# A two-layer token mixer with experts on one core: the stacked keys come by transfer alone, attention values are divided once per tile, and the set-up and all instruction lists are laid out anew

## The chip, the cores and the metric

The kernel runs on one core of one Trainium2 chip. The metric is the device time of one launch in microseconds (us). A tile is 256 tokens; there are 32 of them.

## The reference, cut to what matters

The input x is 2 sequences of 4096 tokens with 512 channels. All is fp32; E is 8 experts, H 16 heads of 32 channels.

```python
def attn(x, Wk, Wr, Wo, time_decay, time_first):      # RWKV
    k = einsum('btc,hc->bth', x, Wk)
    r = einsum('btc,hc->bth', x, Wr)
    y = wkv_scan(-exp(time_decay), time_first, k, r)  # recurrence over the tokens
    return einsum('bth,ch->btc', sigmoid(r) * y, Wo)

def ffn(x, ...):
    h = rmsnorm(x, gamma1)
    q = (h @ Wq + bq).reshape(b, t, H, HD)
    kv = ((h @ Wdown + bdown) @ Wup + bup).reshape(b, t, H, 2 * HD)
    k, v = split(kv, 2, axis=-1)
    att = softmax(einsum('bthd,btgd->bthg', q, k) / sqrt(HD))   # among the 16 heads of one token
    out = einsum('bthg,btgd->bthd', att, v).reshape(b, t, D)
    x = x + (out @ Wo + bo)
    h2 = rmsnorm(x, gamma2)
    gate = softmax(h2 @ Wg + bg)
    return x + einsum('btd,edf,bte->btf', h2, We, gate)

x = x + attn(layernorm(x), ...)
x = x + ffn(layernorm(x), ...)
```

## The kernel before, in words

**Number format.** Each fp32 operand of a product is split into two fp16 halves, hi (written by ScalarE) and lo (the rest, written by VectorE or GpSimd); a product is three passes on TensorE: hi·hi, lo·hi, hi·lo.

**Steps of a tile.** `mix_*` is the first layer: turn the tokens (`mix_turn`), products K and V (`mix_k`, `mix_v`), the recurrence by scans of VectorE in two halves of the channels (`mix_decay`, `mix_sum`, `mix_value`, `mix_scan`, `mix_rec`, `mix_gate`, `mix_split`, each with h = 0 or 1), and the output product (`mix_project`). `att_*` is the attention: `att_turn`, `att_latent`, `att_q`, `att_up`, then for groups of tokens `att_max` (a first product only to get each row's maximum), `att_m`, eight `att_scores` and eight `att_probs`. `fin_*` is the output product, its norm and the gate. `moe`, 16 pieces of 12 products of 512 columns, is the experts; VectorE adds each piece into `acc` (L1311), and TensorE's piece u waits for VectorE's add of piece u-2, because two PSUM banks take turns.

**Stacks.** For the scores, q and k are copied into the tiles `qs` and `ks` with their halves stacked on the partitions: 32 rows each for `qs` = (hi, hi, lo) and `ks` = (hi, lo, hi). SyncE's queue (SP) issues these as DMAs of 64 KB, each of 64-byte pieces, in `att_up`: eight for the two hi copies of q, four for its lo, four for the lo of k. The two hi copies of k are eight copies on VectorE instead, `att_stack` (L1219).

**Attention values.** Each `att_probs(k)` on VectorE takes the reciprocal of four denominators per partition (L1250), adds the two halves of the values (L1251) and multiplies (L1253). `fin_back` turns the result (L1261).

**Order.** Each engine runs a list written out by hand: HEAD, then ORDER once per tile for i = 4 to 30, then TAIL. An entry is (step, part, lag) and works on tile i - lag; in HEAD the third number is the tile itself. So while tile i is mixed, tile i-1 is in attention and tile i-2 in the experts, all interleaved. Nothing but these lists and the semaphores sets the order.

**Set-up.** The weights are loaded, their maxima give powers of two as scales (three phases: k and r; the other projections; the experts), and they are split to hi and lo. Those of k, r and o1 are first turned on TensorE through PSUM banks (`set_turn`, the bank from `turned(n)`). `set_abs` on ScalarE sums absolute values of the experts' blocks as a bound, `set_times` scales them; GpSimd writes their lo half (L686).

Of the kernel before, what the change touches and what calls it, by code (L numbers as in the profile page):

```python
# [122 lines left out]
def att_before(use):  # L123
# [21 lines left out]
    ("att_scores", 5, 0), ("mix_k", 0, 2), ("att_probs", 4, 0), ("att_scores", 6, 0), ("att_probs", 5, 0),
    ("att_scores", 7, 0), ("mix_v", 0, 2), ("att_probs", 6, 0), ("att_probs", 7, 0), ("att_turn", 0, 1),
    ("fin_project", 0, 0), ("att_latent", 0, 1), ("att_q", 0, 1), ("att_up", 0, 1), ("fin_turn2", 0, 0),
    ("fin_gate", 0, 0), ("att_max", 0, 1), ("att_max", 1, 1), ("att_max", 2, 1), ("att_max", 3, 1), ("moe", 0, 0),
    ("moe", 1, 0), ("att_m", 0, 1), ("moe", 2, 0), ("moe", 3, 0), ("att_scores", 0, 1), ("moe", 4, 0),
# [7 lines left out]
    ("att_scores", 7, 3), ("mix_turn", 0, 1), ("moe", 8, 4), ("att_probs", 6, 3), ("att_probs", 7, 3),  # L157
    ("mix_k", 0, 1), ("mix_v", 0, 1), ("att_turn", 0, 2), ("moe", 9, 4), ("moe", 10, 4), ("att_latent", 0, 2),
    ("att_q", 0, 2), ("moe", 11, 4), ("moe", 12, 4), ("att_up", 0, 2), ("fin_project", 0, 3), ("moe", 13, 4),
    ("moe", 14, 4), ("att_max", 0, 2), ("moe", 15, 4), ("fin_turn2", 0, 3), ("att_max", 1, 2), ("att_max", 2, 2),  # L160
    ("moe", 0, 3), ("att_max", 3, 2), ("fin_gate", 0, 3), ("moe", 1, 3), ("att_m", 0, 2), ("moe", 2, 3),
    ("moe", 3, 3), ("att_scores", 0, 2), ("att_scores", 1, 2), ("moe", 4, 3), ("moe", 5, 3), ("att_probs", 0, 2),
    ("att_scores", 2, 2), ("att_probs", 1, 2), ("att_scores", 3, 2), ("moe", 6, 3), ("att_probs", 2, 2),
    ("att_scores", 4, 2), ("moe", 7, 3), ("att_probs", 3, 2), ("att_scores", 5, 2), ("att_probs", 4, 2),
    ("att_scores", 6, 2), ("mix_project", 0, 1), ("att_probs", 5, 2),
# [1426 lines left out]
```

## Time and profile before

| | |
|---|---|
| median of 3 runs | 2910.02 us (2909.48 to 2913.99) |
| the profiled execution | 2906.95 us |
| its span (first to last instruction) | 2905.1 us |
| TensorE busy | 2618.6 us, 90% |
| VectorE busy | 2453.4 us, 84% |
| ScalarE, GpSimd busy | 1522.6 us, 1006.4 us |

PE is TensorE, DVE VectorE, ACT ScalarE, POOL GpSimd, SP SyncE with its DMA queue. Busy time of PE is the union of its matmuls, with modelled ends.

### The profile page before, as it was taken

What the parts mean: (1) busy time and instruction counts of PE and PEld (TensorE: products, weight loads), DVE (VectorE), ACT (ScalarE), POOL (GpSimd) and SP (SyncE); (2) the same over time, 40 slices, a digit from 0 to 9 for tenths busy, and PEclk for the clock granted to TensorE, in tenths of its full rate; (3) what the DMA queues carried; (4) which work ended last, traced back from release to release, by engine and by line L of the source; (5) the groups of instructions that cost most, each with busy time, mean ns of one, the idle gap of its engine ahead of it and who ended that gap; (6) DMA issues with size and microseconds to landing.
All of it is one profiled execution on the core that took longest, in us unless ns stands there. A gap on an engine that the chain in (4) does not pass through costs nothing.

```text
span 2905.1 us, 49052 instructions
## 1 busy us (share of the span) xinstructions
PE 2618.6 (90%) x18896; PEld 1579.7 (54%) x18896; DVE 2453.4 (84%) x4353; ACT 1522.6 (52%) x2783; POOL 1006.4 (35%) x970
## 2 busy tenths in 40 slices
PE   2447999999999999999999999999999999999899
PEld 2324555555556555555655555555555555565454
DVE  5688888889888888988888898888889888888853
ACT  5664555555555555555555555555555555554531
POOL 0354333334333333433333343333333333333320
PEclk9768999999999999999999999999999999999999
DMA  6011111111111101111110111111011111111110
GB/s 213 15 30 30 38 37 16 29 32 37 38 37 32 21 26 35 37 38 38 23 30 23 38 37 37 37 23 28 26 37 38 38 38 22 26 28 37 30 23 15
DMA packets 579083, 102.51 MB, mean 35 GB/s; under 512 B 547346, under 2 KB 547474, under 8 KB 578834
## 3 DMA queue, kind: packets, MB, share of 16 engines
...
## 4 chain that ended last, share of the span: by engine, by line
PE 54%; DVE 32%; ACT 6%; issue 4%; POOL 2%; SPq 1%; DMA 0%; DVEq 0%; ACTq 0%; POOLq 0%
PE bank L1333 49%; DVE wkv L1134 4%; DVE ks L1219 3%; PE bank L1355 3%; DVE acc L1311 3%; DVE zz L1158 2%; DVE wkv L1123 2%; DVE e L1147 2%; DVE ev L1167 2%; DVE on L1253 2%; DVE zz L1130 2%; DVE mcol L1234 1%; DVE h2t L1096 1%; ACT ot L923 1%; DVE hrow L1225 1%
## 5 line engine op out<-in xcount | busy, mean ns | idle before, releaser
L1333 PE MATMUL bank<-w_e,h2t 128*128 128x512 f16 x6144 | 1392.8, 380 | 72.9 <-DVE acc L1311 52.6
L1333 PEld LDWEIGHTS bank<-w_e,h2t 128*128 128x128 f16 x6144 | 587.3, 98 | 754.6 <-DVE acc L1311 77.1
L1311 DVE SCALAR_TENSOR_TENSOR acc<-bank,gates,acc 128x512 f32<-128x512 f32 x512 | 376.6, 741 | 136.6 <-PE bank L1333 132.3
L727 POOL TENSOR_TENSOR pr<-pr 128x512 f16<-128x512 f32 x256 | 307.1, 1200 | 281.9 <-ACT pr L901 279.2
L899 ACT ACTIVATE pr<-bank,plog,col 128x512 f32<-128x512 f32 x256 | 197.1, 770 | 201.0 <-PE bank L1501 201.0
L1134 DVE TENSOR_TENSOR_SCAN wkv<-e,wkv 128x256 f32<-128x256 f32 x256 | 255.9, 1040 | 22.9 <-ACT e L827 19.6
L696 POOL TENSOR_TENSOR zz<-wkv,zz 128x512 f32<-128x512 f32 x64 | 106.7, 1667 | 432.2 <-DVE ev L1145 432.2
L1333 PE MATMUL bank<-w_o,xo 128*128 128x512 f16 x768 | 176.1, 387 | 49.7 <-DVE xo L1096 49.5
L1158 DVE RECIPROCAL zz<-zz 128x256 f32<-128x256 f32 x128 | 218.5, 1729 | 0.0
L901 ACT ACTIVATE pr<-bank,plog,col 128x512 f16<-128x512 f32 x256 | 197.0, 770 | 0.0
L1333 PE MATMUL bank<-xo,w_k 128*128 128x256 f16 x1536 | 175.6, 275 | 12.0 <-DVE xo L1096 12.0
L1234 DVE TENSOR_REDUCE mcol<-bank 128x4 f32<-128x512 f32 x256 | 160.7, 681 | 19.0 <-PE bank L1488 19.0
L1333 PE MATMUL bank<-w_o,oo 128*128 128x512 f16 x768 | 172.6, 382 | 0.9 <-DVE oo L1096 0.9
L1333 PE MATMUL bank<-xo,w_r 128*128 128x256 f16 x1536 | 172.9, 273 | 0.0
L1333 PE MATMUL bank<-ht,w_q 128*128 128x256 f16 x1536 | 172.9, 273 | 0.0
L1333 PEld LDWEIGHTS bank<-xo,w_k 128*128 128x128 f16 x1536 | 149.2, 99 | 31.6 <-DVE xo L1096 12.9
L1333 PEld LDWEIGHTS bank<-ht,w_q 128*128 128x128 f16 x1536 | 150.3, 98 | 17.4
L1333 PEld LDWEIGHTS bank<-xo,w_r 128*128 128x128 f16 x1536 | 150.2, 98 | 17.4
L1333 PEld LDWEIGHTS bank<-w_o,xo 128*128 128x128 f16 x768 | 73.7, 99 | 141.9 <-DVE xo L1096 55.2
L709 POOL TENSOR_TENSOR x<-x,bo_row 128x512 f32<-128x512 f32 x64 | 92.5, 1466 | 161.8 <-ACT x L854 161.8
L743 POOL TENSOR_TENSOR acc<-x,x 128x512 f32<-128x512 f32 x64 | 80.3, 1276 | 173.1 <-DMA result<-acc 173.1
L714 POOL TENSOR_TENSOR qo<-t,qo 128x256 f16<-128x256 f32 x128 | 109.4, 862 | 84.6 <-ACT qo L884 84.6
...
## 6 DMA issues: line engine op xcount, KB each, us to landing
...
ks<-k SPq DMA_DIRECT2D x128, 64.0 KB, 2.4
...
```

The lines of the kernel that those rows point to most:

```text
L696: nc.gpsimd.tensor_tensor(zz[:, :, :], wkv[:, 2, :, 0:T], zz[:, :, :], ALU.add).then_inc(mix_pool.sem, 1)
L709: nc.gpsimd.tensor_tensor(x2[:, s, :], x2[:, s, :], bo_row[:, :], ALU.add).then_inc(att_pool.sem, 1)
L714: nc.gpsimd.tensor_tensor(grouped(dst, 1)[:, :, b, :], t32[:, b % 2, :].rearrange("p (g j) -> p g j", g=G), grouped(dst, 0)[:, :, b, :], A ...
L727: nc.gpsimd.tensor_tensor(pr16[:, 1, k % 2, :], pr[:, k % 2, :], pr16[:, 0, k % 2, :], ALU.subtract).then_inc(att_pool.sem, 1)
L899: nc.scalar.activation(pr[:, k % 2, :], att_bank[ATT_BANK["S", k]][:, :], ACT.Exp, bias=plog[:, 0:1], scale=colof["soft"])\
L901: nc.scalar.activation(pr16[:, 0, k % 2, :], att_bank[ATT_BANK["S", k]][:, :], ACT.Exp, bias=plog[:, 0:1], scale=colof["soft"])\
L1134: V.tensor_tensor_scan(wkv[:, n, c, 1:T + 1], e1[:, c, :], src[:, c, :], wkv[:, n, c, 0:1], ALU.mult, ALU.add).then_inc(mix_dve.sem, 1)
L1158: V.reciprocal(zz[:, c, :], zz[:, c, :]).then_inc(mix_dve.sem, 1)
L1219: V.tensor_copy(ks[n * HD:(n + 1) * HD, :, f, :], grouped(k16, 0)[f * HD:(f + 1) * HD].rearrange("p g b j -> p g (b j)")).then_inc(att_dve ...
L1234: V.tensor_reduce(mcol[:, 4 * k:4 * k + 4], att_bank[ATT_BANK["M", k]][:, :].rearrange("p (g x) -> p g x", g=4), AX, ALU.max).then_inc(att ...
L1311: V.scalar_tensor_tensor(out=acc[:, s, :], in0=moe_bank[u % 2][:, :], scalar=gates[:, s, e:e + 1], in1=acc[:, s, :], op0=ALU.mult, op1=ALU ...
L1333: ins = nc.tensor.matmul(dst, left(a), right(b), start=(n == 0), stop=(n == last))
```

## The change

1. `att_stack` is gone from VectorE. SP's `att_up` issues eight more DMAs per tile, for rows 0 and 2 of `ks`, between q's lo and k's lo.
2. `att_probs` only adds the two halves, with the denominator as a 33rd column. `fin_back` does one reciprocal of 32 columns and one multiply of 1024 per tile.
3. `set_load` is in five parts, `set_experts` in eight. The turned weights use six PSUM banks in turn in place of two. The bounds of o1 and o2 come from sums of absolute values on ScalarE (four more `set_abs`), no longer from maxima on VectorE.
4. The lists of all five engines have new entries; one line of them is shown.

```diff
-MAXED = ["k", "r", "o1", "q", "o2", "small", "experts"]
+MAXED = ["k", "r", "q", "small", "experts"]
+SUMMED = ["o1", "o2"] + [f"e{e}" for e in range(E)]
+TURN_BANKS = [0, 1, 4, 5, 6, 7]
...
 DVE_HEAD = [
-    ("set_scale", 0, -1), ("set_max", 2, -1), ("set_k", 0, -1), ("set_k", 1, -1), ("set_max", 3, -1),
+    ("set_scale", 0, -1), ("mix_turn", 0, 0), ("set_k", 0, -1), ("set_k", 1, -1), ("set_r", 0, -1), ("set_r", 1, -1),
...
 def turned(n):
-            return bank[n % 2][:, :]
+            return bank[TURN_BANKS[n % len(TURN_BANKS)]][:, :]
...
-        stack_in = Steps(sem("stack_in"), 16, qk=16)
+        stack_in = Steps(sem("stack_in"), 16, qk=24)
...
 def att_up(t, _):                      # SP
-                for src, dst, name, first in ((qo16, qs, "q", (0, 1)), (k16, ks, "k", ())):
-                    rest = 2 if first else 1
+                for src, dst, name, first in ((qo16, qs, "q", (0, 1)), (k16, ks, "k", (0, 2))):
+                    rest = 3 - sum(first)
...
 def set_max(_, n):                     # DVE
                 if name == "small":
+                    dve.wait_ge(summed, 2 * CB)
...
-            def att_stack(t, _):
-                dve.wait_ge(*att_act.done(t, "k"))
-                for f in range(4):
-                    for n in (0, 2):
-                        V.tensor_copy(ks[n * HD:(n + 1) * HD, :, f, :],
-                                      grouped(k16, 0)[f * HD:(f + 1) * HD].rearrange("p g b j -> p g (b j)")).then_inc(att_dve.sem, 1)
...
 def att_probs(t, k):                   # DVE
-                V.reciprocal(rden[:, 4 * k:4 * k + 4], pv[:, :, HD]).then_inc(att_dve.sem, 1)
-                V.tensor_reduce(og, pv.rearrange("p g (l d) -> p g d l", l=2)[:, :, 0:HD, :], AX, ALU.add).then_inc(att_dve.sem, 1)
-                dve.wait_ge(*att_dve.done(t, "norm", 3 * k + 1))
-                V.tensor_tensor(og, og, rden[:, 4 * k:4 * k + 4].unsqueeze(2).to_broadcast([P, 4, HD]), ALU.mult).then_inc(att_dve.sem, 1)
+                V.tensor_reduce(on[:, 4 * k:4 * k + 4, :], pv.rearrange("p g (l d) -> p g d l", l=2), AX, ALU.add).then_inc(att_dve.sem, 1)
...
 def fin_back(t, _):                    # DVE
+                V.reciprocal(rden[:, :], on[:, :, HD]).then_inc(fin_dve.sem, 1)
+                dve.wait_ge(*fin_dve.done(t, "den"))
+                V.tensor_tensor(on[:, :, 0:HD], on[:, :, 0:HD], rden[:, :].unsqueeze(2).to_broadcast([P, G, HD]), ALU.mult).then_inc(fin_dve.sem, 1)
+                dve.wait_ge(*fin_dve.done(t, "quot"))
```

What the lists do to the order, at three places. First TensorE, within one tile of the steady part, from the query product (w_q) to the gate product (w_g): `w_e` are experts' pieces of 12, `w_u` is `att_up`, `w_o<-oo` is `fin_project`, `ident,ot` is `fin_turn2`, `ks,qs` of 8 is one `att_max`. Before:

```order
L1333 MATMUL bank<-ht,w_q 128x256 x48
L1333 MATMUL bank<-w_e,h2t 128x512 x24
L1471 MATMUL bank<-c,w_u 128x256 x16
L1333 MATMUL bank<-w_o,oo 128x512 x24
L1333 MATMUL bank<-w_e,h2t 128x512 x24
L1488 MATMUL bank<-ks,qs 128x128 x8
L1333 MATMUL bank<-w_e,h2t 128x512 x12
L1355 MATMUL bank<-ident,ot 128x128 x8
L1488 MATMUL bank<-ks,qs 128x128 x16
L1333 MATMUL bank<-w_e,h2t 128x512 x12
L1488 MATMUL bank<-ks,qs 128x128 x8
L1333 MATMUL bank<-w_g,h2t 128x8 x24
```

And of the change:

```order
L1333 MATMUL bank<-ht,w_q 128x256 x48
L1333 MATMUL bank<-w_e,h2t 128x512 x12
L1471 MATMUL bank<-c,w_u 128x256 x16
L1333 MATMUL bank<-w_e,h2t 128x512 x24
L1333 MATMUL bank<-w_o,oo 128x512 x24
L1333 MATMUL bank<-w_e,h2t 128x512 x36
L1355 MATMUL bank<-ident,ot 128x128 x8
L1487 MATMUL bank<-ks,qs 128x128 x16
L1333 MATMUL bank<-w_g,h2t 128x8 x24
L1333 MATMUL bank<-w_e,h2t 128x512 x12
L1487 MATMUL bank<-ks,qs 128x128 x16
```

The first use of the stacks (`ks,qs`) moved behind all experts' pieces of the older tile and behind the turn, and only half of it stands ahead of the gate.

Second VectorE, in the same stretch: from the gated output's second operand to the add of pieces 14 and 15. `ks<-k` is `att_stack`, `wkv<-wcol` to `zz<-e` is `mix_decay`, `mcol` is `att_max`. Before:

```order
L1118 COPY wkv<-carry 128x6
L1123 SCALAR_TENSOR_TENSOR wkv<-wcol,wkv,xk 128x256 x2
L1126 TENSOR_TENSOR e<-xk,wkv 128x512
L1130 TENSOR_SCALAR zz<-e,ucol 128x256 x2
L1219 COPY ks<-k 32x32x32 x8
L1225 STREAM_TRANSPOSE hrow<-ht 128x1024
L1271 SCALAR_TENSOR_TENSOR x<-bank,col,x 128x512 x2
L1311 SCALAR_TENSOR_TENSOR acc<-bank,gates,acc 128x512
L1229 TENSOR_TENSOR vp<-hrow,vp 128x32x32
L1234 TENSOR_REDUCE mcol<-bank 128x4 x2
L1311 SCALAR_TENSOR_TENSOR acc<-bank,gates,acc 128x512 x2
L1096 SCALAR_TENSOR_TENSOR h2t<-bank,h2t 128x512 x2
```

And of the change:

```order
L1225 STREAM_TRANSPOSE hrow<-ht 128x1024
L1311 SCALAR_TENSOR_TENSOR acc<-bank,gates,acc 128x512 x2
L1104 SCALAR_TENSOR_TENSOR xo<-ev,col,xo 128x512
L1229 TENSOR_TENSOR vp<-hrow,vp 128x32x32
L1271 SCALAR_TENSOR_TENSOR x<-bank,col,x 128x512 x2
L1311 SCALAR_TENSOR_TENSOR acc<-bank,gates,acc 128x512
L1126 COPY wkv<-carry 128x6
L1131 SCALAR_TENSOR_TENSOR wkv<-wcol,wkv,xk 128x256 x2
L1134 TENSOR_TENSOR e<-xk,wkv 128x512
L1138 TENSOR_SCALAR zz<-e,ucol 128x256 x2
L1311 SCALAR_TENSOR_TENSOR acc<-bank,gates,acc 128x512 x2
L1104 SCALAR_TENSOR_TENSOR h2t<-bank,h2t 128x512 x2
```

The copies are gone, and the transpose of the values and the output's add (L1271) now stand ahead of the second half's `mix_decay`.

Third VectorE at the start of the program: the first tile's lo half (`xo<-bank`). Before, it stands behind the experts' scales (`ee`):

```order
L1090 SCALAR_TENSOR_TENSOR w_o<-bank,scl,w_o 128x512 x4
L1004 TENSOR_TENSOR mx<-mx,gam 128x4 x8
L977 TENSOR_REDUCE bound<-mx 128x8
L1079 TENSOR_SCALAR pw<-bound 128x8
...
L1038 TENSOR_SCALAR ee<-pw 128x8 x2
L1096 SCALAR_TENSOR_TENSOR xo<-bank,xo 128x512 x2
```

And of the change:

```order
L1060 TENSOR_SCALAR wcol<-ecol 128x4
L1104 SCALAR_TENSOR_TENSOR xo<-bank,xo 128x512 x2
L1098 SCALAR_TENSOR_TENSOR w_k<-bank,scl,w_k 128x512 x4
L1098 SCALAR_TENSOR_TENSOR w_r<-bank,scl,w_r 128x512 x4
...
L984 TENSOR_REDUCE mx<-bvcol 128x1
L1012 TENSOR_TENSOR mx<-mx,gam 128x4 x3
L984 TENSOR_REDUCE bound<-mx 128x9
L1126 COPY wkv<-carry 128x6
```

It moved to right behind the first scales, and the first tile's recurrence begins behind the second phase's bounds instead of behind the experts'. The loads keep their order on SP up to the constants; then come the first two experts, the first residual, four experts, the second tile's x (which waits for the first tile's second `mix_decay`), and only then the last two experts.

## Rows read from the trace of the kernel before

**Rows 1.** The chain that ended last, by line, over the whole run.

```profile
PE bank L1333 49%; DVE wkv L1134 4%; DVE ks L1219 3%; PE bank L1355 3%; DVE acc L1311 3%; DVE zz L1158 2%; DVE wkv L1123 2%; DVE e L1147 2%; DVE ev L1167 2%; DVE on L1253 2%; DVE zz L1130 2%; DVE mcol L1234 1%; DVE h2t L1096 1%; ACT ot L923 1%; DVE hrow L1225 1%
```

**Rows 2.** Stretches: length, busy of PE, PEld, DVE, ACT, POOL, clock, DMA share, GB/s.

```profile
0.00:258.19 258.19, 109.14 (x794) 80.91 (x795) 182.86 (x343) 155.46 (x310) 86.61 (x90) 0.79 0.28 77
258.19:2696.00 2437.81, 2319.34 (x16887) 1398.29 (x16886) 2146.30 (x3789) 1297.00 (x2346) 867.37 (x827) 1.00 0.16 32
2696.00:2858.86 162.86, 147.93 (x1004) 81.21 (x1003) 109.58 (x200) 69.92 (x127) 49.97 (x51) 0.97 0.15 25
```

**Rows 3.** Timeline of PE: start, length; a turn, an expert piece, a query product.

```profile
1019.49 1.09 PE L1355 MATMUL bank<-ident,ot 128*128 128x128 f32 x8 [0.21 <-ACT ot L923]
...
1022.21 2.77 PE L1333 MATMUL bank<-w_e,h2t 128*128 128x512 f16 x12 [0.74 <-DVE h2t L1096]
...
1078.52 5.40 PE L1333 MATMUL bank<-ht,w_q 128*128 128x256 f16 x48
```

**Rows 4.** What PE waited for, 258.19 to 2696: us in total, times, longest.

```profile
PE bank L1333 <- DVE acc L1311: 52.6, 55, 2.0
PE bank L1512 <- DVE on L1251: 22.2, 28, 0.8
PE bank L1333 <- DVE h2t L1096: 21.8, 28, 1.5
PE bank L1333 <- DVE xo L1096: 13.9, 27, 0.5
```

**Rows 5.** Groups, 300 to 2700: busy us, mean ns, then idle before them.

```profile
L1311 DVE SCALAR_TENSOR_TENSOR acc<-bank,gates,acc 128x512 f32<-128x512 f32 x450 | 330.6, 740 | 77.2 <-PE bank L1333 73.3 <-issue 0.7
L1134 DVE TENSOR_TENSOR_SCAN wkv<-e,wkv 128x256 f32<-128x256 f32 x228 | 228.6, 1043 | 12.2 <-ACT e L827 9.1
L1158 DVE RECIPROCAL zz<-zz 128x256 f32<-128x256 f32 x113 | 193.2, 1730 | 0.0
L1234 DVE TENSOR_REDUCE mcol<-bank 128x4 f32<-128x512 f32 x224 | 141.0, 681 | 18.8 <-PE bank L1488 18.8
L1253 DVE TENSOR_TENSOR on<-on,rden 128x128 f32<-128x128 f32 x224 | 115.3, 515 | 7.7
L1219 DVE COPY ks<-k 32x1024 f16<-32x1024 f16 x224 | 94.3, 421 | 6.1
L1147 DVE TENSOR_TENSOR e<-e,v 128x512 f32<-128x512 f32 x57 | 65.6, 1152 | 0.0
L1250 DVE RECIPROCAL rden<-bank 128x4 f32<-128x4 f32 x224 | 37.8, 169 | 0.4 <-PE bank L1513 0.4
L1229 DVE TENSOR_TENSOR vp<-hrow,vp 128x1024 f16<-128x1024 f32 x28 | 34.1, 1218 | 0.0
```

**Rows 6.** Timeline of SP's queue in one tile: start, length of the issuing.

```profile
1085.90 5.65 SPq L648 DMA_DIRECT2D qs<-qo  x8
...
1094.46 2.82 SPq L652 DMA_DIRECT2D ks<-k  x4
```

**Rows 7.** The stretch of that burst, columns as in rows 2.

```profile
1087.00:1098.00 11.00, 11.00 (x60) 5.76 (x59) 9.99 (x19) 6.12 (x13) 3.36 (x5) 1.00 0.75 90
```

**Rows 8.** Start of the program on DVE and POOL: timeline, idle before.

```profile
34.70 0.16 DVE L977 TENSOR_REDUCE mx<-bqcol 128x1 f32<-128x4 f32 x1 [3.78 <-DMA bg_row<-in_ffn_bg]
65.33 1.29 DVE L1096 SCALAR_TENSOR_TENSOR xo<-bank,xo 128x512 f16<-128x512 f32 x2
71.86 1.40 DVE L1123 TENSOR_TENSOR_SCAN wkv<-wcol,wkv,xk 128x256 f32<-128x256 f32 x2 [0.27 <-ACT xk L807]
...
189.40 4.50 POOL L686 TENSOR_TENSOR w_e<-w_e 128x512 f16<-128x512 f32 x4
```

**Rows 9.** Start of the program on PE: timeline.

```profile
112.50 7.98 PE L1333 MATMUL bank<-w_o,xo 128*128 128x512 f16 x24 [33.53 <-DVE xo L1096]
177.14 1.03 PE L1501 MATMUL bank<-qs,ks 106*128 106x128 f16 x8 [3.57 <-DMA qs<-m]
258.19 6.84 PE L1333 MATMUL bank<-w_e,h2t 128*128 128x512 f16 x24
```

More of the change, by code:

```diff
@@ L145 @@
[L145 to L149, printed above, removed]
@@ new lines @@
+    ("att_probs", 6, 0), ("att_probs", 7, 0), ("mix_k", 0, 2), ("att_turn", 0, 1), ("mix_v", 0, 2),
+    ("att_latent", 0, 1), ("att_q", 0, 1), ("fin_project", 0, 0), ("att_up", 0, 1), ("fin_turn2", 0, 0),
+    ("fin_gate", 0, 0), ("att_max", 0, 1), ("att_max", 1, 1), ("att_max", 2, 1), ("moe", 0, 0), ("att_max", 3, 1),
+    ("moe", 1, 0), ("moe", 2, 0), ("att_m", 0, 1), ("moe", 3, 0), ("moe", 4, 0), ("att_scores", 0, 1),
+    ("att_scores", 1, 1), ("moe", 5, 0), ("att_probs", 0, 1), ("att_scores", 2, 1), ("moe", 6, 0),
@@ L154 @@
+    ("att_probs", 1, 1), ("att_scores", 3, 1), ("att_probs", 2, 1),
 ]
 PE_ORDER = [
[L157 to L165, printed above, removed]
+    ("att_scores", 4, 3), ("moe", 7, 4), ("att_probs", 3, 3), ("att_scores", 5, 3), ("moe", 8, 4),
@@ new lines @@
+    ("moe", 9, 5), ("mix_turn", 0, 2), ("att_probs", 6, 4), ("att_probs", 7, 4), ("moe", 10, 5), ("mix_k", 0, 2),
+    ("mix_v", 0, 2), ("att_turn", 0, 3), ("fin_project", 0, 4), ("att_latent", 0, 3), ("att_q", 0, 3),
+    ("att_up", 0, 3), ("moe", 11, 5), ("moe", 12, 5), ("moe", 13, 5), ("fin_turn2", 0, 4), ("moe", 14, 5),
+    ("moe", 15, 5), ("fin_gate", 0, 4), ("att_max", 0, 3), ("att_max", 1, 3), ("att_max", 2, 3), ("att_max", 3, 3),
+    ("moe", 0, 4), ("att_m", 0, 3), ("moe", 1, 4), ("moe", 2, 4), ("moe", 3, 4), ("att_scores", 0, 3),
@@ new lines @@
+    ("att_latent", 0, 2), ("att_q", 0, 2), ("att_up", 0, 2), ("fin_project", 0, 3), ("moe", 12, 4), ("moe", 13, 4),
+    ("moe", 14, 4), ("moe", 15, 4), ("fin_turn2", 0, 3), ("fin_gate", 0, 3), ("att_max", 0, 2), ("att_max", 1, 2),
+    ("att_max", 2, 2), ("att_max", 3, 2), ("moe", 0, 3), ("att_m", 0, 2), ("moe", 1, 3), ("moe", 2, 3),
+    ("att_scores", 0, 2), ("att_scores", 1, 2), ("moe", 3, 3), ("att_probs", 0, 2), ("att_scores", 2, 2),
+    ("att_probs", 1, 2), ("att_scores", 3, 2), ("moe", 4, 3), ("att_probs", 2, 2), ("att_scores", 4, 2),
@@ L225 @@
+    ("att_vlo", 0, 1), ("mix_split", 0, 2), ("mix_decay", 1, 2), ("fin_turn2", 0, 0), ("att_max", 0, 1),
 ]
 DVE_ORDER = [
[L228 to L231 removed]
@@ new lines @@
+    ("att_stats", 0, 3), ("att_norm", 0, 3), ("moe", 10, 5), ("fin_back", 0, 4), ("mix_decay", 0, 2),
+    ("att_turn", 0, 3), ("mix_sum", 0, 2), ("mix_value", 0, 2), ("att_latent", 0, 3), ("fin_project", 0, 4),
+    ("mix_scan", 0, 2), ("mix_rec", 0, 2), ("mix_rec", 1, 2), ("moe", 11, 5), ("mix_gate", 0, 2), ("moe", 12, 5),
+    ("moe", 13, 5), ("mix_split", 0, 2), ("mix_decay", 1, 2), ("att_vt", 0, 3), ("moe", 14, 5), ("moe", 15, 5),
+    ("mix_sum", 1, 2), ("fin_turn2", 0, 4), ("att_vlo", 0, 3), ("att_max", 0, 3), ("att_max", 1, 3),
```

435 lines of the change are left out of this document (213 added, 222 removed), and 3 rows, old and new, of the table POOL_HEAD.

## The prediction

> **What bounds the kernel now.** First the chain that ended last [rows 1]: half of it is the experts' products on PE, but the rest is a string of VectorE lines, each 1 to 4%, among them the key copies `ks` with 3% and the divided values `on` with 2%. So neither engine bounds alone; they take turns. Next the busy time by stretch [rows 2]. Up to 258.19 us, where the first expert piece of tile 0 starts [rows 9], PE works 109 of 258 us: that is the filling. From there to 2696 PE is busy 2319.3 of 2437.8 us, so 118.5 are idle. Tile 9's first piece starts at 1022.21 [rows 3], so a tile takes (1022.21 - 258.19) / 9 = 84.9 us, the stretch holds 28.7 tiles, and a tile is 80.8 us of work and 4.1 of idle. That 4.1 is all that a better order can win per tile. Who ends the idle [rows 4], over 28: the adds into `acc` 1.9, `on` 0.8, `h2t` 0.8, `xo` 0.5 us, and 0.1 to 0.2 of small ones. Every large one is VectorE being late. Its busy time in the same stretch is 2146 us, 74.8 a tile [rows 2].
>
> **VectorE's work.** Per tile the change removes the eight copies, 94.3 / 28 = 3.4 us, the reciprocals, 37.8 / 28 = 1.35, and the multiplies, 115.3 / 28 = 4.1 [rows 5]. It adds one reciprocal of 32 columns: between the 128x4 (0.17) and the 128x256 one (1.73) the slope is 6.2 ns a column, so 0.34 us; one multiply of 1024 columns, nearest row the 128x1024 subtraction with 1.22 us; the eight adds have 33 values for 32, 0.1 together. Net -7.2 us. This is no gain by itself: it counts only where PE waits for VectorE, at most the 4.1.
>
> **Where the multiply goes.** The old 128x128 multiply averages 515 ns, more than a twelfth of the 1218 ns row per column, eight times within the scores' phase, in which GpSimd writes the lo halves. The Trainium skill, "SBUF — State Buffer", section on the two separate sides, says that a VectorE operation with two SBUF inputs and a GpSimd one exclude each other for the whole instruction; the excess fits it. By that rule the new multiply, which stands where GpSimd is mostly idle, costs 1.2 and not 8 x 0.5; the sum has 1.2 either way, from its row.
>
> **The stacks.** SP issues 24 transfers in place of 16. Eight took 5.65 us and the last four 2.82, so one is 0.70 us [rows 6], and eight more are 5.65. The query product ended at 1078.52 + 5.40 = 1083.9 [rows 3], SP began 2.0 later. The new list has `mix_exp` and `att_latent` of ScalarE ahead of q after a later V product, which I put at 0.7 more. Landing is then 2.7 + 24 x 0.70 + 1.5 = 21.0 us after the query product; the 1.5 is from the last issue (1097.3) to the end of that burst's traffic, with DMA at 0.75 to 1098 [rows 7]. PE has before its first use of the stacks: six expert pieces of 2.6 (2.77 less the overlap with the next), `att_up` 1.8 (16 products where q's 5.40 has 48), `fin_project` 5.2 (24 of a piece's products), the turn 1.0 [rows 3], together 23.6. The slack is 2.6 us: hidden, but it is the thinnest cover of the change. Nothing else in SP's queue is hurt: the x load and the store come after.
> A page speaks against these transfers: the Trainium skill, "DMA: Bandwidth & Descriptors", Specifications, wants 512 bytes or more for line rate, and these are 64-byte pieces. The trace agrees on the rate, 90 GB/s in the burst; by the rate alone 24 x 64 KB would take 17.5 us, about what issuing takes, so the sum stays.
>
> **The decisive stretch.** It runs from the end of `h2t`'s lo half, T. PE before: gate, moe 0, then on. PE after, from T to the start of piece 5: gate 0.6, five pieces 13.0, four `att_max` halves 0.9, `att_m` and two scores 0.7 = 15.2. VectorE after, to the add of piece 3, which piece 5 needs: two maxima 1.4 twice and once more twice (8 x 0.68 less overlap = 5.1), gate 1.7 (eight small operations, the smallest row being 0.17), four adds 3.0, first scans 1.4 to 2.1, `att_m` 0.6, value products 1.3 to 1.8 = 13.1 to 14.3. In time. Then scans 2.1 to 3.1, reciprocal 1.73, add 0.74 [rows 5]: 17.7 to 19.9 (21 with GpSimd in the way as in the 1152 ns row), against PE's start of piece 6 at 15.2 + 2.6 + 0.45 = 18.25. Wait 0 to 2.5, I take 1.0 where before it was 1.9. After that each step has a slack of 0.3 to 2 us. `h2t` keeps its 0.8: turn, ScalarE, VectorE in a row with the same 0.9 of maxima as cover. For `on`, `xo`, the start of the next tile and the store (now behind an x load, which leaves it a slack of about 0.3 before `acc` is needed) I put 0.7 together, bounds 0.2 to 1.5. Sum 2.5 us of idle a tile, bounds 1.1 to 4.1. Gain 1.6 x 28.7 = 46 us, bounds 0 to 86.
>
> **The filling.** Tile 0's lo half waits at 65.33 behind all expert loads, and its scans start at 71.86 [rows 8]. In the new list what holds them is the last constant, at 34.70 [rows 8], so about 35.5: 36 earlier. From there on ScalarE has seven pairs of expert sums ahead of tile 0's tanh (+3), and its sums of the last two experts, loaded only after tile 0's second `mix_decay`, come ahead of the second tanh: tile 0's output product starts near 80 instead of 112.50 [rows 9], 32 earlier. Three weight splits moved behind it cost 5.1, the longer stack 5.7. GpSimd then has five experts in a row (4.50 each [rows 8] and 0.6 for ScalarE's hi before it, 26 us) ahead of tile 1's denominators; with these the first scores start near 151 instead of 177.14: 26 earlier. From the first scores to the first expert piece were 81.1 us [rows 9]; the new order needs about 66 plus some waits, I take 71. So the first piece is 36 us earlier, near 222. Bounds: 18 (the expert chain of ScalarE and GpSimd runs on into the scores) and 48 (66 us, no waits).
>
> **The end.** 2696 to 2858.86 has 14.9 us of PE idle [rows 2]. Less VectorE work gives 3 back; but in the tail list tile 29 has only four pieces, the turn and the gate between its query product and its stacks (about 16 us against 21) and tile 30 has 19: +4. Net +1, bounds -5 to +8.
>
> **Sum.** 46 + 36 - 1 = 81 us off 2906.95, 2826 for such an execution; the runs' median stands 3.1 above it, so 2829.
>
> **Rivals.**
> (a) VectorE's stretch stays as late as before, as the new POOL list puts `mix_num` before the first scores' lo: idle stays 4.1, 2875. For it: the acc waits moved, not removed, have only 0.3 to 1.5 us of slack. Against: 3.4 us of copies are gone from right before the stretch.
> (b) The order comes out as planned, idle falls to 1.1, and the filling gives 42: 2910 - 86 - 42 + 1 = 2783.
> (c) The stacks land 2 us beyond the slack each tile, because ScalarE ends q late: +57, 2886. It decides from 2.6 us.
> (d) Slower: 24 transfers in one queue do not keep 0.70 us but take 0.95 each, landing 6.0 later, 3.4 beyond the slack and 97 us in sum, and the filling gives only its 18: 2910 - 46 - 18 + 97 + 1 = 2944. It needs over 0.90 us each to eat the gain. Against: no growth from the first eight to the last four [rows 6], and the DMA share of 0.75 leaves room [rows 7].
> (e) The filling gives nothing since the expert chain ends when it did: 2865.
>
> **Numbers.** Likeliest 0.50, own range 2795 to 2860; (a) 0.13; (b) 0.15; (c) 0.11; (d) 0.05; (e) 0.06. The range 2780 to 2884 takes in (b), (a), (e) and the likeliest, and leaves out most of (c) and (d). A measurement of this kernel tells about 0.2% from no change, 5.8 us: faster 0.93, same 0.02, slower 0.05.
>
> **What would show it.** Right: per tile near 83.3 us; L1219 gone, no wait of PE for `ks` in the steady stretch; acc waits near 1 us a tile, at piece 6; VectorE busy near 68 a tile; first expert piece near 222. Wrong: PE waiting for DMA `ks`; a tile over 84; the first piece after 240; SP rows of k's hi above 6 us for eight.

## The result, and the profile after

| | before | after |
|---|---|---|
| time, median of 4 runs, us | 2910.86 (2909.48 to 2913.99) | 2759.11 (2758.60 to 2760.13) |
| profiled execution: span, us | 2905.1 | 2756.5 |
| first expert piece of tile 0, us | 258.19 [rows 9] | 229.15 |
| a tile in the steady stretch, us | 85.05 | 80.58 |

The changed kernel takes 0.9478 of the time before, 95% interval 0.9461 to 0.9494: 151.8 us less, where 81 were forecast and 2780 was the range's lower end. Direction right, size wrong by 70 us. A tile is the mean of 22, between the 7th and the 29th start of the first layer's output product. Times here and below are medians of undisturbed executions; the profile of `maxima_first` alone is of a disturbed one, and none of its rows is read.

The page of the changed kernel, busy time and then the chain that ended last, by engine:

```profile
PE 2586.4 (94%) x18896; PEld 1580.4 (57%) x18896; DVE 2133.6 (77%) x3647; ACT 1531.3 (56%) x2799; POOL 948.9 (34%) x970
...
PE 88%; DVE 4%; ACT 4%; POOL 2%; SPq 1%; issue 1%; DMA 0%; ACTq 0%; DVEq 0%; POOLq 0%
```

VectorE is nearly out of the chain: what was a string of its lines [rows 1] is 4% now, and PE bounds. The stretches, columns as in [rows 2]:

```profile
0.00:229.15 229.15, 101.09 (x785) 76.80 (x786) 157.04 (x310) 163.07 (x333) 87.88 (x90) 0.74 0.38 95
229.15:2578.57 2349.42, 2317.23 (x17046) 1417.20 (x17045) 1885.78 (x3186) 1315.35 (x2374) 818.74 (x839) 1.00 0.23 40
```

This stretch has 32 us of idle, but its first and last tiles are longer than the others. The split per tile is read from the 22 even tiles, before and then after, both with the same number of matmuls (589 a tile):

```profile
625.71:2496.85 1871.14, 1777.28 (x12958) 1072.31 (x12959) 1655.53 (x2905) 996.10 (x1805) 669.47 (x638) 1.00 0.16 32
580.22:2353.09 1772.87, 1755.48 (x12962) 1075.37 (x12960) 1437.21 (x2421) 1000.19 (x1805) 622.41 (x638) 1.00 0.23 40
```

Divided by 22, PE's busy time was 80.8 us a tile and is 79.8, its idle was 4.3 and is 0.8. So 3.5 came from idle and 1.0 from time that the trace counts as busy. Who ends the idle in the longer stretch, as in [rows 4]:

```profile
PE bank L1333 <- DVE h2t L1104: 25.0, 29, 3.4
PE bank L1333 <- DVE acc L1311: 1.8, 2, 1.2
```

`on` and `xo` are gone, the `acc` waits (52.6) nearly, and only `h2t` is as it was: 0.74 us a tile. One tile on PE: two starts of the output product, one period apart; between them the query product, the first use of the stacks, the gate, piece 0 and what follows it, and pieces 5 and 6:

```profile
902.56 5.34 PE L1333 MATMUL bank<-w_o,xo 128*128 128x512 f16 x24
...
924.49 5.40 PE L1333 MATMUL bank<-ht,w_q 128*128 128x256 f16 x48
...
953.07 1.06 PE L1487 MATMUL bank<-ks,qs 104*128 104x128 f16 x16
954.87 0.76 PE L1333 MATMUL bank<-w_g,h2t 128*128 128x8 f16 x24 [0.74 <-DVE h2t L1104]
955.49 2.75 PE L1333 MATMUL bank<-w_e,h2t 128*128 128x512 f16 x12
958.08 1.06 PE L1487 MATMUL bank<-ks,qs 104*128 104x128 f16 x16
...
969.89 2.75 PE L1333 MATMUL bank<-w_e,h2t 128*128 128x512 f16 x12
...
973.13 2.75 PE L1333 MATMUL bank<-w_e,h2t 128*128 128x512 f16 x12
...
983.14 5.34 PE L1333 MATMUL bank<-w_o,xo 128*128 128x512 f16 x24
```

Piece 0 ends at 958.24, and the product behind it starts 0.16 us before that. By these modelled ends work that follows without a wait overlaps with what is ahead of it; work that follows a wait does not.

The decisive stretch in that tile, on VectorE and on GpSimd beside it:

```profile
966.24 0.67 DVE L1155 TENSOR_TENSOR e<-e,v 128x512 f32<-128x512 f32 x1
...
967.79 1.44 DVE L1142 TENSOR_TENSOR_SCAN wkv<-e,wkv 128x256 f32<-128x256 f32 x2
...
969.35 1.74 DVE L1166 RECIPROCAL zz<-zz 128x256 f32<-128x256 f32 x1
971.01 0.65 DVE L1311 SCALAR_TENSOR_TENSOR acc<-bank,gates,acc 128x512 f32<-128x512 f32 x1
```

```profile
966.39 1.65 POOL L703 TENSOR_TENSOR zz<-wkv,zz 128x512 f32<-128x512 f32 x1 [3.94 <-DVE ev L1153]
969.31 1.09 POOL L707 TENSOR_TENSOR ev<-wkv,ev 128x512 f32<-128x512 f32 x1 [1.27 <-DVE wkv L1142]
```

The add that piece 6 needs is done at 971.66, and PE comes for it at 973.13: VectorE is 1.5 us early, and this is its slack there. Groups of the steady stretch, where [rows 5] had 1043, 1152 and 8 x 515 ns:

```profile
L1142 DVE TENSOR_TENSOR_SCAN wkv<-e,wkv 128x256 f32<-128x256 f32 x228 | 185.6, 855 | 66.3 <-ACT e L834 65.4
L1155 DVE TENSOR_TENSOR e<-e,v 128x512 f32<-128x512 f32 x57 | 52.1, 915 | 0.0
L1259 DVE TENSOR_TENSOR on<-on,rden 128x1024 f32<-128x1024 f32 x30 | 36.8, 1225 | 1.0
L1257 DVE RECIPROCAL rden<-on 128x32 f32<-128x32 f32 x30 | 10.4, 347 | 0.0
```

SP's queue in that tile, as in [rows 6], and the start on PE, as in [rows 9]:

```profile
932.24 5.65 SPq L655 DMA_DIRECT2D qs<-qo  x8
...
940.79 6.73 SPq L655 DMA_DIRECT2D ks<-k  x8
947.56 2.81 SPq L659 DMA_DIRECT2D ks<-k  x4
```

```profile
81.79 8.30 PE L1333 MATMUL bank<-w_o,xo 128*128 128x512 f16 x24 [46.88 <-DVE xo L1104]
...
140.63 3.79 PE L1487 MATMUL bank<-ks,qs 104*128 104x128 f16 x32 [18.71 <-DMA ks<-k]
...
158.86 1.04 PE L1500 MATMUL bank<-qs,ks 106*128 106x128 f16 x8 [2.83 <-DMA qs<-m]
...
222.60 1.97 PE L1355 MATMUL bank<-ident,ot 128*128 128x128 f32 x8 [11.45 <-ACT ot L930]
```

The issuing ends 20.5 us after the query product (929.89), PE's first use is 23.2 after it, without a wait. This tile is one of 6 in 32 in which the keys' first eight took over 6 us; in the others they took 5.6 to 5.9.

### The profile page after: what moved, and what is told of

It reads as the page before. It is cut to its first block, busy times and chain, and to the rows that moved or that the text cites. A ratio compares the mean times of both kernels' runs of the same rounds, so it can differ in the third digit from the quotient of the medians.

```text
span 2756.5 us, 48625 instructions
## 1 busy us (share of the span) xinstructions
PE 2586.4 (94%) x18896; PEld 1580.4 (57%) x18896; DVE 2133.6 (77%) x3647; ACT 1531.3 (56%) x2799; POOL 948.9 (34%) x970
## 4 chain that ended last, share of the span: by engine, by line
PE 88%; DVE 4%; ACT 4%; POOL 2%; SPq 1%; issue 1%; DMA 0%; ACTq 0%; DVEq 0%; POOLq 0%
PE bank L1333 78%; PE bank L1355 3%; PE bank L1500 2%; PE bank L1471 2%; PE bank L1511 2%; DVE h2t L1104 1%; PE bank L1487 1%; POOL w_e L693 1%; ACT h2t L939 1%; PE bank L1512 1%; ACT ot L789 1%; DVE mcol L1234 0%; ACT t L888 0%; POOL pr L734 0%; DVE acc L1311 0%
## 5 line engine op out<-in xcount | busy, mean ns | idle before, releaser
L734 POOL TENSOR_TENSOR pr<-pr 128x512 f16<-128x512 f32 x256 | 295.7, 1160 | 182.3 <-ACT pr L908 180.9
L1142 DVE TENSOR_TENSOR_SCAN wkv<-e,wkv 128x256 f32<-128x256 f32 x256 | 210.8, 864 | 74.6 <-ACT e L834 73.4
L750 POOL TENSOR_TENSOR acc<-x,x 128x512 f32<-128x512 f32 x64 | 80.3, 1276 | 261.5 <-DMA result<-acc 261.5
L1249 DVE TENSOR_REDUCE on<-bank 128x132 f32<-128x264 f32 x256 | 103.3, 424 | 74.3 <-PE bank L1512 74.3
L703 POOL TENSOR_TENSOR zz<-wkv,zz 128x512 f32<-128x512 f32 x64 | 94.1, 1470 | 158.4 <-DVE ev L1153 158.3
```

What stands on the lines that cost most here:

```text
L703: nc.gpsimd.tensor_tensor(zz[:, :, :], wkv[:, 2, :, 0:T], zz[:, :, :], ALU.add).then_inc(mix_pool.sem, 1)
L734: nc.gpsimd.tensor_tensor(pr16[:, 1, k % 2, :], pr[:, k % 2, :], pr16[:, 0, k % 2, :], ALU.subtract).then_inc(att_pool.sem, 1)
L1142: V.tensor_tensor_scan(wkv[:, n, c, 1:T + 1], e1[:, c, :], src[:, c, :], wkv[:, n, c, 0:1], ALU.mult, ALU.add).then_inc(mix_dve.sem, 1)
L1249: V.tensor_reduce(on[:, 4 * k:4 * k + 4, :], pv.rearrange("p g (l d) -> p g d l", l=2), AX, ALU.add).then_inc(att_dve.sem, 1)
```

## The experiments

Theory at this point: the operations unload VectorE, the lists turn that into time and cover the longer transfers; idle of PE costs more than the trace shows as idle. Rivals: the operations alone carry it; or the lists alone. The period is the mean of the same 22 tiles in every kernel, with PE's busy and idle time in it; a wait is idle of over 0.15 us ahead of an instruction of PE.

**Operations and lists apart.** `ops_only` is the kernel before with both operations and its own lists; `division_only_old_lists` has the division alone; the others start from the changed kernel and put one or both old operations back. One line of each is shown; with the copies go 16 transfers again:

```
 DVE lists:    ("att_vt", ..)  ->  ("att_stack", ..), ("att_vt", ..)             copies_back
-(k16, ks, "k", (0, 2))                     +(k16, ks, "k", ())
-V.tensor_reduce(on[..], pv.., AX, ALU.add)                                    # division_back
+V.reciprocal(rden[..], pv[:, :, HD]); V.tensor_reduce(og, ..); V.tensor_tensor(og, og, rden.., ALU.mult)
```

> The kernel before with the two changed operations alone (both key copies by transfer, one division a tile); its own lists, two turning banks and set-up, the copies' entries dropped from the lists. Theory 1, the operations carry the steady gain: VectorE's 7.2 us a tile are what PE waited for, idle falls from 4.1 to near 1 and the tile to 80.6 to 81.5, with nothing from the filling: 2785 to 2815. Theory 2, the lists carry it: h2t's, xo's and most acc waits stay where the old order puts them, the tile stays near 83 to 83.5: 2850 to 2875. A first expert piece near 258 either way.

> The kernel before with one division a tile and nothing else: copies on VectorE, 16 transfers, old lists. With both operations it was 3018, with PE waiting 4.1 us a tile for the transferred keys. Theory 1, that loss was the longer transfer queue alone, and VectorE's relief is worth something by itself: the `on` waits of 0.8 a tile go and the acc waits shrink, tile 83.5 to 84.3, 2865 to 2890. Theory 2, the relief is worth nothing without a new order: 2905 to 2913.

> The changed kernel with the eight key copies back on VectorE (3.4 us a tile, ahead of the V transpose) and 16 stack transfers. Theory A, VectorE has slack under the new lists (it idles 16 of 80.6 us a tile): under 0.5 us a tile, 2755 to 2775. Theory B, each us taken off VectorE came back as time: 3.4 x 28 = 95 us, near 2850. In between, if the stretch behind the copies (value products, fin's x2, decay, the turn) has under 3.4 us of slack: 1 to 2 us a tile, 2790 to 2815.

> The changed kernel with reciprocal and multiply per four heads again, in the scores' phase. It adds 3.8 us of VectorE a tile there at the old durations, where VectorE waits 2.2 us a tile for the PV products. Theory A, slack: under 1 us a tile, 2760 to 2785. Theory B, one for one: 2860. If the small multiplies take 0.5 us because GpSimd writes the probabilities' lo halves in the same phase, their row reads 450 ns or more again under these lists; if it was the old order's doing, under 300.

> The changed kernel with both old operations back, so set-up, banks and lists alone. Theory 2, the lists carry the gain: 2780 to 2810. Theory 1, the operations carry it: 2860 or more, the filling's 29 us being all that stays. If both are needed, that is if the lists only pay when VectorE is 7 us shorter, this one and the one with operations alone each lose more than half of the gain of 151: both above 2835.

| kernel | lists | division | keys | us | period | busy | idle | waits a tile |
|---|---|---|---|---|---|---|---|---|
| before | old | old | copied | 2910.86 | 85.05 | 80.8 | 4.3 | 6 |
| `division_only_old_lists` | old | new | copied | 2861.04 | 83.17 | 80.2 | 2.9 | 4 |
| `ops_only` | old | new | transferred | 3018.15 | 88.75 | 81.9 | 6.9 | 4 |
| `lists_only` | new | old | copied | 2830.23 | 82.46 | 80.5 | 2.0 | 4 |
| `copies_back` | new | new | copied | 2796.63 | 81.33 | 80.0 | 1.3 | 2 |
| `division_back` | new | old | transferred | 2793.94 | 81.68 | 80.3 | 1.4 | 3 |
| after | new | new | transferred | 2759.11 | 80.58 | 79.8 | 0.8 | 1 |

Most of these missed their theories. `division_only_old_lists` came 4 us under theory 1, `lists_only` between its two, `division_back` 9 above theory A and far from B; `copies_back` is in the range of its middle case, though its tile is 0.74 longer and not 1 to 2. Both theories for `ops_only` missed: it is 107 us slower than before. First PE's waits in its stretch 258 to 2696, then one tile's first use of the keys:

```profile
PE bank L1477 <- DMA ks<-k: 111.9, 27, 4.7
```

```profile
1046.10 0.62 PE L1477 MATMUL bank<-ks,qs 104*128 104x128 f16 x8 [4.68 <-DMA ks<-k]
```

The query product ended there at 1024.14, so the keys land 22.0 after it, while the old list brings PE to them after 17.3. The transfers that cost 157 us under the old lists (3018 against 2861) win 36 and 37.5 under the new ones (2830 to 2794, 2797 to 2759). That is rival (c) and (d)'s place, with another cause: no slower transfers, but a list that reaches for them too early. PE waits 4.2 us a tile for them, and the period is 5.6 longer than without the transfers; the granted clock, at 0.98 in these tiles, has a part in the rest. The division, in contrast, pays under either: 50 us under the old (its `on` and `xo` waits are gone, its `acc` waits still 53.1), 34 and 35 under the new. Set-up, banks and lists with the old operations are worth 81, with the first expert piece at 236.8 where it was 258.2. No run takes these three apart. So neither rival holds: the lists alone give 81 of the 152, the two operations behind them 71, and the two operations without them lose 107.

So theory A, slack, fell for both operations under the new lists as well, and so did B: 3.4 us of copies a tile cost 0.74, 3.8 us of division 1.09. The busy time goes with the waits: 79.8 with one a tile, 80.0 with two, 80.2 to 80.5 with three or four, 80.8 with six. The multiply is 535 ns a piece in `division_back`. Which of them are long is seen with GpSimd's queue beside them:

```profile
908.64 0.72 DVE L1253 TENSOR_TENSOR on<-on,rden 128x128 f32<-128x128 f32 x1
...
911.37 0.29 DVE L1253 TENSOR_TENSOR on<-on,rden 128x128 f32<-128x128 f32 x1
```

```profile
907.71 2.67 POOL L734 TENSOR_TENSOR pr<-pr 128x512 f16<-128x512 f32 x2 [1.88 <-ACT pr L908]
911.53 1.16 POOL L734 TENSOR_TENSOR pr<-pr 128x512 f16<-128x512 f32 x1 [1.15 <-ACT pr L908]
```

0.29 alone, 0.72 while GpSimd works. Copies are hit too: tile 0's eight take 9.03 us in `copies_back` for 3.4, GpSimd being at the experts, and its first piece comes at 236.1 in place of 229.2.

**The slack of the stacks.**

```
-for f, n: sp.dma_start(ks[n.., :, f, :], k16 block f)
+for f, n: two transfers, groups 0 to 15 and 16 to 31          # 32 in place of 24, the same bytes
```

> The changed kernel with each of the eight transfers of the key's hi half issued as two of half the size, so 32 stack transfers in place of 24 with the same bytes. It measures the slack of the stacks under the new lists: the query product's end to PE's first use is 23.2 us, and with the old lists 24 transfers land 22.0 after it. Theory 1, the slack is 1.2 us and an issue costs what it did whatever its size (0.70): landing 5.6 later, PE waits for the keys 4.4 us a tile, 2760 + 125 = 2885. Theory 2, an issue costs by its pieces (0.35 for half the size): nothing changes, 2760. By the forecast's slack of 2.6 and a full 0.70 each: 3.0 a tile, 2845.

Measured: 2908.34, 23 us above theory 1. Sixteen half transfers take as long each as whole ones, and PE waits 99.1 us in 27 tiles, 3.7 each. Issuing ends 25.2 after the query product where it was 20.1 (means of 21 tiles), so the slack was 5.1 - 3.7 = 1.4 us, not 2.6; the 1.2 ahead of this run was close. First SP's row and PE's wait in one tile, then PE's clock in two stretches of 4 us behind it, the last column but two:

```profile
1493.42 10.76 SPq L656 DMA_DIRECT2D ks<-k  x16
```

```profile
1508.77 1.65 PE L1488 MATMUL bank<-ks,qs 104*128 104x128 f16 x16 [3.42 <-DMA ks<-k]
```

```profile
1508.00:1512.00 4.00, 3.23 (x43) 2.54 (x44) 2.76 (x6) 1.44 (x3) 0.00 (x0) 0.63 0.86 205
1512.00:1516.00 4.00, 4.00 (x30) 2.22 (x29) 0.90 (x6) 0.22 (x1) 2.42 (x2) 0.94 0.19 70
```

After 3.4 us of idle the granted clock falls to the lower of its two levels (1.2 of 2.4 GHz) for about 3 us, by the two means. The period is 85.1 us, 4.5 more for 3.7 of wait.

**The slack of VectorE, and what a wait costs.** Unused reciprocals (1.73 each) behind the second scans, ahead of the add that piece 6 needs, two and then one:

```
 mix_scan, h == 1:   +for c in range(2): V.reciprocal(e2[:, c, :], v32[:, HF + c, :])
```

> The changed kernel with two more 128x256 reciprocals on VectorE (3.47 us a tile, results not used) behind the second scans, in the decisive stretch, ahead of the add that piece 6 waits for. The profile gives that add a slack of 1.5 us there. Theory 1, slack as read: PE waits about 2.0 us a tile at piece 6 and the tile is 82.7, 2760 + 60 = 2820. Theory 2, lateness feeds itself because a late VectorE meets GpSimd's probabilities' lo halves again (scans above 950 ns on average): 3.5 or more a tile, above 2860. Theory 3, the slack behind takes it all up: under 2775.

> The changed kernel with one more 128x256 reciprocal (1.73 us a tile, result not used) where vector_delay had two. With two the wait at piece 6 was 1.99, so the slack is 3.47 - 1.99 = 1.48. Theory 1, one leaves a wait of 0.25 plus about 0.15 of drain a tile and the granted clock stays at its full value: tile 80.9 to 81.1, 2768 to 2776. Theory 2, any wait there is amplified as with two (2.8 us for 2.0): 0.35 to 0.4 and no more, the same numbers, but with the clock under 1.00 in the steady stretch. Theory 3, lateness of VectorE as such costs what it costs with two, half of 85: 2800.

Measured 2844.31 and 2777.55. PE's rows at piece 6: two tiles with two reciprocals, the clock behind the second of them, and a tile with one:

```profile
1419.80 2.76 PE L1336 MATMUL bank<-w_e,h2t 128*128 128x512 f16 x12 [1.94 <-DVE acc L1314]
...
1502.46 4.36 PE L1336 MATMUL bank<-w_e,h2t 128*128 128x512 f16 x12 [1.92 <-DVE acc L1314]
```

```profile
1504.00:1508.00 4.00, 4.00 (x33) 2.10 (x32) 3.31 (x5) 0.63 (x1) 0.00 (x0) 0.64 0.00 0
```

```profile
1544.59 2.76 PE L1335 MATMUL bank<-w_e,h2t 128*128 128x512 f16 x12 [0.30 <-DVE acc L1313]
```

One leaves a wait of 0.30, so the slack was 1.43, as read. A typical tile takes 81.06, 0.48 more: the wait costs 0.18 beyond itself, near the 0.16 of overlap that it takes away. With two the wait is 1.9 on average and the period 83.4, 2.8 more, between theories 1 and 2. The two rows tell why: behind 1.94 us of idle the clock stays and the tile takes 82.7, 2.1 more for 1.9 of wait, as a short wait would; behind 1.92 it falls, piece 6 takes 4.36 us in place of 2.75 and the tile 84.4. It fell in 11 of 25 tiles, and nothing in the rows tells which. The scans stay at 858 ns, so theory 2 with its GpSimd is out.

**GpSimd beside the scans.**

```
 mix_sum (GpSimd), h == 1, behind the denominators (not shown: waits for pr16 to be free, and for the two to be done):
+for c in range(2): nc.gpsimd.tensor_tensor(pr16[:, 1, c, :], wkv[:, 2, :, 0:T], wkv[:, 2, :, 0:T], ALU.subtract)
```

> The changed kernel with two more 128x512 subtractions on GpSimd (2.3 us a tile, results not used) behind the second denominators, where the second scans of VectorE run (two in 1.44 us; before, 3.13 with GpSimd at work beside them). Theory 1, the two engines keep each other out: the second scans' mean rises from 855 to about 1100 ns (the pair by 1.0 to 1.7 us), piece 6 loses most of its 1.5 us slack, 2760 to 2790. Theory 2, the old length came from something else in the old order: the mean stays within 20 ns, 2760.

Measured 2786.97, in the range of theory 1, but by another wait than the one it names. VectorE's second scans, GpSimd beside them, and what PE then waits for:

```profile
1548.58 2.47 DVE L1149 TENSOR_TENSOR_SCAN wkv<-e,wkv 128x256 f32<-128x256 f32 x2
```

```profile
1549.08 2.80 POOL L709 TENSOR_TENSOR pr<-wkv 128x512 f16<-128x512 f32 x2
```

```profile
1554.31 0.19 PE L1518 MATMUL bank<-vp,pr 128*128 128x66 f16 x1 [0.95 <-POOL pr L741]
```

The pair takes 2.47 for 1.44, as theory 1 has it; the mean over both halves rises only to 942, since the first pair is untouched. Piece 6 has the slack for it; of the 28 us, 24 are the wait for the first probabilities' lo half (28 times in the steady stretch), which stands behind the two subtractions. So this run shows that GpSimd lengthens the scans, and not what longer scans cost. PE's busy time stays at 79.8 here with two waits a tile: at that place no product overlapped before either (piece 5 ends at 972.64 in the changed kernel, the next product starts at 972.69). The page of the Trainium skill "SBUF — State Buffer", section on the two separate sides, says that of a VectorE operation with two SBUF inputs and a GpSimd one that reads SBUF, the one that starts first holds the shared port for its whole instruction. The scans agree: they take 1.09 and 1.46 us one by one, the second ending 0.55 behind the subtraction that had started before it.

**The one wait left.** Piece 0 ahead of the gate in the steady list, its blocks 0 and 1 waiting for the first half of `h2t` only:

```
-("att_max", 1, 2), ("fin_gate", 0, 3), ("moe", 0, 3),
+("att_max", 1, 2), ("moe", 0, 3), ("fin_gate", 0, 3),
+ahead = {2 * b: fin_dve.done(t, "h2_lo", b) for b in range(2)}       # waited for ahead of blocks 0 and 2
```

> The changed kernel with expert piece 0 ahead of the gate's product in the steady list, its first half waiting only for the first lo half of h2t and its second half for the second. PE's one wait left, 0.74 us for h2t, and the 0.15 of drain behind it go; the gate comes 2.4 us later on PE, but VectorE was at the maxima until 0.4 us before. Theory 1, the wait is what is left to win: the tile falls by 0.8, 2735 to 2742. Theory 2, VectorE's adds are then late by the gate's shift and piece 2 waits for add 0: the same within 3 us, 2757 to 2763.

Measured 2748.29 (2742.94 to 2748.93), ratio to before 0.9437 (0.9423 to 0.9451): the fastest of the kernels run (two below are within 0.5 us of it), 11 us below the changed one, half of what theory 1 gave. PE's row:

```profile
1513.01 2.75 PE L1335 MATMUL bank<-w_e,h2t 128*128 128x512 f16 x12 [0.23 <-DVE h2t L1104]
```

The wait is 0.23 and not zero, because the first lo half itself ends there, and the period is 80.15, 0.43 less and not 0.8.

**The filling.** Four turning banks in place of six; then, step by step, what is ahead of tile 0's first scores: expert splits 5 to 7 behind them on GpSimd, with ScalarE's hi halves of 6 and 7 later too (`late_experts`), the maxima ahead of tile 1's sums on VectorE (`maxima_first`, alone), both and ScalarE's normalised rows earlier (`filling_reordered`), ScalarE's last scalings behind the scores too (`scalings_late`). Three of these also with piece 0 first.

```
-TURN_BANKS = [0, 1, 4, 5, 6, 7]            +TURN_BANKS = [0, 1, 4, 5]
 POOL_HEAD: -.. ("set_e5", ..), ("set_e6", ..), ("mix_sum", 1, 1), ..    # late_experts
            +.. ("att_scores", 7, 0), .. ("set_e5", ..), ("att_stats", 0, 1), ("set_e6", ..), ("set_e7", ..)
 DVE_HEAD:  -("mix_sum", 1, 1), ("att_max", 3, 0), ("att_m", 0, 0)       # maxima_first
            +("att_max", 3, 0), ("att_m", 0, 0), ("mix_sum", 1, 1)
```

> The changed kernel with four turning banks in place of six. With six, PE turns the first weights without a wait by 23.8 us, but tile 0's output product starts at 81.79 and waits for VectorE all the time since. Theory 1, VectorE's and ScalarE's own work up to there sets that start and the banks only let PE be early: within 2 us, 2757 to 2761. Theory 2, earlier turning starts the splits earlier: the output product 4 to 10 us later, 2763 to 2769.

> The changed kernel with the splits of experts 5, 6 and 7 behind the first scores on GpSimd (and the hi halves of 6 and 7 on ScalarE later too), and ScalarE's exponentials of tile 1's second half ahead of expert 5's. Theory 1, the expert chain on GpSimd, which runs without a pause from 128.3 to 159.1 us, is what holds the first scores' lo halves and so the filling's missing 7 us: the first scores' product at 150 to 153 in place of 158.9, the first expert piece at 219 to 224 in place of 229.2, 2748 to 2754. Theory 2, the stacks' landing at 140.6 and what follows it set the filling: within 2 us of 2759.

> The changed kernel with VectorE's second half sums of tile 1 behind tile 0's last maxima and `att_m` in the filling, instead of ahead of them, where they wait 3.05 us for ScalarE. Theory 1, this order holds tile 0's scores: their product starts at 151 to 153 in place of 158.86. Theory 2, GpSimd's expert chain to 159.1 holds the lo halves anyway: the first probabilities' product stays at 165, and the time within 2 us of 2759.

> late_experts plus the maxima first on VectorE and tile 0's normalised rows ahead of the last expert scalings on ScalarE. All three holds of the first scores that the profile shows are gone: the stacks at 141 are then the first limit, the scores' product at 150 to 152, the first probabilities' product near 156 in place of 165.3. If that passes through to the end, 8 us: near 2751. If experts 6 and 7, now split while tile 1's latents are made, take it back (in late_experts the turn of tile 0's output waited 3.4 us longer and came 2.3 later), 2756 to 2761.

> filling_reordered with ScalarE's scalings of experts 6 and 7 and the hi halves of expert 5 moved behind the first scores as well (7 us of ScalarE). Theory 1, they were the last hold of the probabilities: the first probabilities' product at 157 to 159 in place of 164.1 and the first expert piece 5 to 6 us earlier than 231.5: 2752 to 2756. Theory 2, from the scores on the filling is set by other work (ScalarE between tile 1's keys and tile 0's norms, and the 24 transfers of tile 1, which end at 224.5 in the changed kernel): the probabilities come earlier, the first piece does not, 2758 to 2762.

> Both: expert splits late and piece 0 ahead of the gate. If the filling and the steady stretch add up, 2748 less what the late experts gave: 2737 to 2744 by theory 1, 2746 to 2750 by theory 2.

> The same with piece 0 ahead of the gate in the steady list: 10 to 11 us below filling_reordered, so 2740 if the filling gives its 8 us, 2746 to 2750 if it doesn't.

> The same with piece 0 ahead of the gate in the steady list: 10 to 11 us below scalings_late by either theory, 2742 to 2746 by theory 1, 2747 to 2751 by theory 2.

| | us | scores' product | first probabilities | turn of tile 0's output |
|---|---|---|---|---|
| after | 2759.11 | 158.86 | 165.27 | 222.60 |
| `four_turn_banks` | 2759.17 | 158.14 | 164.53 | 220.92 |
| `late_experts` | 2760.58 | 158.19 | 164.32 | 224.93 |
| `maxima_first` | 2760.56 | not read | | |
| `filling_reordered` | 2760.33 | 154.64 | 164.10 | 224.86 |
| `scalings_late` | 2759.21 | 154.42 | 160.47 | 222.72 |

With piece 0 first: 2748.67, 2750.18 and 2748.72. Kernels with one and the same filling place the first expert piece between 227.5 and 230.1, so less than some 2 us in this table says nothing. Not one of these steps moves the time, though the last brings the probabilities 4.8 us forward. PE in `scalings_late`:

```profile
160.47 0.21 PE L1520 MATMUL bank<-vp,pr 128*128 128x66 f16 x1 [5.01 <-POOL pr L732]
...
222.72 1.97 PE L1364 MATMUL bank<-ident,ot 128*128 128x128 f32 x8 [12.93 <-ACT ot L928]
...
229.34 4.01 PE L1342 MATMUL bank<-w_e,h2t 128*128 128x512 f16 x12
```

Tile 1's output product starts at 170.69, 4.8 us earlier than in the changed kernel, and the turn of tile 0's output waits for ScalarE until 222.7 all the same. What is won ahead of the scores is taken back behind them.

## Why the prediction was right or wrong

The measured 2759 lies below the range and below every rival. Counted from expert piece to expert piece, tile 27's was at 2553.28 and is at

```profile
2406.02 2.75 PE L1333 MATMUL bank<-w_e,h2t 128*128 128x512 f16 x12
```

So the 27 tiles from tile 0's took 2295.1 us and take 2176.9: 118 won where 1.6 x 27 = 43 were forecast, 75 more. The filling gave 7 less than forecast, what lies behind tile 27's piece as much as forecast, and the step from an execution to the median is 0.5 us here where 3.1 were taken: together the 70. Of the 75, some 46 are waits that did not come, some 27 are busy time, and 2 are long tiles of the kernel before (85.0 a tile, not 84.9).

- **"Wait 0 to 2.5, I take 1.0" at piece 6, and 0.7 for `on`, `xo` and the rest**: the largest miss, by size. Both are near zero, the idle is 0.8 and not 2.5: 1.7 x 27 = 46 us. The scans were put at 2.1 to 3.1 and took 1.44, the add was done at T + 16.9 (T is 954.8) and not 17.7 to 19.9, while PE's arrival at T + 18.3 was as forecast. The surcharge on the scans was GpSimd's presence, carried over from rows of the old order. `gpsimd_in_the_way` puts it back, and `lists_only`, with the scans at 852 ns and the old operations, shows that the lists removed it. In its idle this was rival (b)'s case, 0.8 for its 1.1; (b)'s filling of 42 did not come.
- **"That 4.1 is all that a better order can win per tile"**: this step failed in kind, not only in size. A tile's 80.8 us of work were taken as fixed; they are 79.8, and the whole gain is 4.4. A wait takes away the overlap of 0.16 as well, and the surplus counts as busy in the trace: `vector_delay_half` measures 0.18 for one wait. PE had 6 waits a tile (those of [rows 4] are 4.9 of them), now one: 5 x 0.18 = 0.9 of the 1.0. The kernels between have busy times between, with 0.14 to 0.25 for each wait; that all of the 1.0 is this overlap is worked out so, not isolated. Worth 1.0 x 27 = 27 us.
- **"VectorE's work", net -7.2**: its terms are right (reciprocal 347 ns for 340, multiply 1225 for 1220). VectorE's busy time fell from 75.3 to 65.3 a tile, 2.7 more than that, of which the eight scans, shorter by 0.19 each, are 1.5. That it "counts only where PE waits" held: 7.2 us less work under the new lists are worth 82.46 - 80.58 = 1.9.
- **"Where the multiply goes"**: right, 1.2 for 8 x 0.5.
- **"The stacks", slack 2.6**: right in sign, too large. PE's way was 23.2 and not 23.6, the landing near 21.9 and not 21.0, and the slack is 1.2 to 1.4. "SP rows of k's hi above 6 us for eight", one of its signs of being wrong, did show, in 6 of 32 tiles, without a wait. "It is the thinnest cover of the change" is what `split_transfers` and `ops_only` show at 149 and 157 us. The wait of rivals (c) and (d) is what comes as soon as the list or the queue changes.
- **"The filling", 36**: 29 came. The output product was right (81.79 for "near 80"), the scores 8 late (158.86 for 151), and the 71 us behind them were 70.3. But that 71 is no fixed distance: `scalings_late` moves the scores and the probabilities, and the first piece stays. What sets its place is open: in the stretch before it ScalarE takes tile 1's keys and values ahead of tile 0's squares, and PE waits 11.45 us for the turn; the issuing of tile 1's transfers ends at 224.5. Neither was tried. The longer stack did bring the keys 4.5 later (140.63 against 136.13 in `copies_back`), near its 5.7, but as a net cost it was wrong in sign: with the copies back the scores are 3.9 and the first piece 6.9 later.
- **"The end", net +1**: behind tile 27's first piece the kernel took 351.8 us and takes 350.5. The 1.7 steady tiles in that should have brought 1.7 x 4.38 = 7.4, so the end cost 6, inside its bounds of -5 to +8.
